# A hybrid attention and feed-forward kernel: the set-up gets a semaphore per part, its work is spread over other engines, and the planner's costs are replaced

## The reference, cut to what matters

```
x = x + attn_a(layernorm(x))     # causal, 16 heads of 16, biases, Wp
x = x + ffn(layernorm(x))        # silu(x Wg) * (x Wu), then Wd; integer weights / 127
x = x + attn_b(layernorm(x))     # sliding window of 64 keys, 16 heads; no biases
x = x + ffn(layernorm(x))        # the same ffn weights again
```

## Time and profile before

| | us |
|---|---|
| median of 3 runs | 1241.68 |
| lowest and highest | 1239.53, 1243.46 |
| the profiled execution | 1242.7 |
| its span, first to last instruction | 1240.9 |
| PE busy | 1107.1 (89%) |
| DVE busy | 830.3 (67%) |
| ACT busy | 725.8 (58%) |
| POOL busy | 385.0 (31%) |

### The profile page before, as it was taken

How to read it: one execution, slowest core, us unless ns; L and a number is a source line. 1 busy time by engine, 2 the same in 40 slices (tenths; PEclk the granted TensorE clock), 3 DMA queues, 4 the chain that set the end, 5 groups by cost and what they waited for, 6 DMA issues and landing times.

```text
span 1240.9 us, 32317 instructions
## 1 busy us (share of the span) xinstructions
PE 1107.1 (89%) x13339; PEld 670.4 (54%) x13339; DVE 830.3 (67%) x1547; ACT 725.8 (58%) x1038; POOL 385.0 (31%) x385
## 2 busy tenths in 40 slices
PE   4788888998998888999998888899899888899997
PEld 2542336765864224765685332676586422476675
DVE  7788935565687881666688893566568888256652
ACT  2257783566455777456645677456645577745653
POOL 7343223212343324202432322321233332420242
PEclk9889999999999999999999999999999999999999
DMA  7430000122223000113212200012222200011101
GB/s 281 135 134 16 11 11 23 56 74 72 75 71 109 16 11 10 46 58 103 71 36 72 100 12 11 23 56 70 72 79 71 76 16 11 11 46 52 57 19 35
DMA packets 70385, 71.64 MB, mean 58 GB/s; under 512 B 26016, under 2 KB 62304, under 8 KB 69344
## 3 DMA queue, kind: packets, MB, share of 16 engines
q1 hardware_dynamic: 70240, 69.56, 17.0%
HBM read 23.60 MB, written 8.39 MB: 26 GB/s over the span
## 4 chain that ended last, share of the span: by engine, by line
PE 67%; DVE 16%; ACT 7%; issue 4%; POOL 4%; DMA 1%; POOLq 0%; ACTq 0%; DVEq 0%
PE ring L1692 12%; PE ring L1724 7%; PE ring L1659 7%; PE ring L1725 7%; DVE peak L1254 5%; PE ring L1614 5%; ACT probs_causal L1450 4%; PE ring L1738 4%; PE ring L1743 4%; PE ring L1567 3%; DVE xn L1147 2%; PE ring L1568 2%; PE ring L1569 2%; DVE peak_c L1254 2%; POOL h_lo L1122 2%
## 5 line engine op out<-in xcount | busy, mean ns | idle before, releaser
L1254 DVE TENSOR_REDUCE peak<-ring 128x2 f32<-128x1024 f32 (+5 forms) x320 | 324.2, 1032 | 73.1 <-PE ring L1636 30.5
L1450 ACT ACTIVATE probs_causal<-ring 128x1024 f32<-128x1024 f32 (+1 forms) x320 | 286.6, 939 | 128.0 <-PE ring L1659 97.5
L1659 PE MATMUL ring<-q_st,k_st 64*64 64x192 f16 (+5 forms) x2752 | 166.0, 296 | 26.8 <-ACT probs_causal L1450 15.3
L1122 POOL TENSOR_TENSOR h_lo<-h_f,h_hi 128x512 fp32r<-128x512 f32 x96 | 122.9, 1289 | 193.0 <-ACT h_hi L1484 193.0
L1692 PE MATMUL ring<-probs_causal,V 128*32 128x512 f32 (+3 forms) x1536 | 166.5, 511 | 5.5 <-POOL probs_causal L1107 5.0
L1107 POOL TENSOR_SCALAR_AFFINE_SELECT probs_causal<-probs_causal 128x512 f32<-128x512 f32 x128 | 80.9, 635 | 281.9 <-ACT probs_causal L1450 281.7
L1724 PE MATMUL ring<-xf_hi,w_gu_sb 128*128 128x512 f32 x384 | 155.6, 405 | 7.4 <-DVE xf_lo L1154 6.6
L1113 POOL TENSOR_TENSOR onf<-osb,onf 128x512 f32<-128x512 f32 x64 | 81.6, 1276 | 241.1 <-DVE onf L1297 241.1
L1725 PE MATMUL ring<-xf_lo,w_gu_sb 128*128 128x512 f32 x384 | 150.5, 392 | 0.0
L1659 PEld LDWEIGHTS ring<-q_st,k_st 64*64 64x64 f16 x2752 | 65.9, 105 | 154.0 <-ACT probs_causal L1450 57.5
L1322 DVE SCALAR_TENSOR_TENSOR h_f<-ring,gate 128x512 f32<-128x512 f32 x96 | 65.9, 690 | 121.2 <-PE ring L1725 64.1
(11 more groups left out here) (154 smaller groups left out, 1986.4 us busy)
## 6 DMA issues: line engine op xcount, KB each, us to landing
q_st<-q_part SPq DMA_DIRECT2D x96, 128.0 KB
w_qkv<-img_qkv SPq DMA_DIRECT2D x7, 1536.0 KB, 7.7
on_lo<-onf SPq DMA_DIRECT2D x64, 128.0 KB, 2.6
k_st<-k_part SPq DMA_DIRECT2D x48, 144.0 KB, 2.1
k_st<-k_part SPq DMA_DIRECT2D x48, 128.0 KB, 2.1
y<-X SPq DMA_DIRECT2D x8, 512.0 KB, 3.0
wp_sb<-img_wp SPq DMA_DIRECT2D x7, 512.0 KB, 3.4
x_next<-in_x SPq DMA_DIRECT2D x3, 1024.0 KB, 6.2
```

Of the source, the lines that this page charges most:

```text
L1122: pool.tensor_tensor(h_lo[m][:], h_f[m][:], h_hi[m][:].bitcast(F32), ALU.subtract).then_inc(h_lo_done, 1)
L1254: dve.tensor_reduce(dst, scores, AX.X, ALU.max).then_inc(a_max, 1)
L1450: act.activation(in_banks(block[0:rows, n % slots], unit, w), heads_of(flat_of(a, e), unit, w)[0:rows], ACT.Exp, scale=back[a % 2]).then_i ...
L1659: last = pe.matmul(psum[BLOCK * m:BLOCK * m + BLOCK, r, per * n:per * n + w], keys[rows_of(r), head, first_key + BLOCK * m:first_key + BLO ...
```

## The change

The change has four parts.

1. `s_pool` is replaced by a semaphore for each part: `s_ident`, `s_rows`, `s_masks`, `s_xt_edges`, `s_onf`, and `s_v_ones` for all of the ones in `V`. POOL makes the identity first. PE starts when the identity and its bfloat16 copy are there; ACT starts at once. The rows for the stacks are made in one column and copied to 575 more. Each later user waits for its own part.
2. ACT fills the ones of `V` and the zeros of `onf` (two instructions at its start), which POOL did. The values' part of the first attention's weights is no longer scaled and split with the rest: a new event `values` splits it as soon as it has landed (ACT, POOL). The ten warm-up matmuls on PE after the first event are gone; the five ahead of it stay. The load of `bias_qk` is issued second in place of fourth.
3. POOL's residual adds (`x`) and its low parts of the gate and up weights (`gu`, last step) now wait until the second half of x is normalised.
4. The planner's costs, its delays, `LANDED`, `SOON` (0.3 to 0.15), `TABLE_LOAD` and the times at which the engines become free are replaced. The table `TIMES` gets one row more, for `values`, and is otherwise the same. All lists are made anew from this.

Cut to its core:

```
-TABLE_LOAD = 1.5
-UNITS, SOON, TURN, RELOAD = 2, 0.3, 2.0, 6.0
+TABLE_LOAD = 1.42
+UNITS, SOON, TURN, RELOAD = 2, 0.15, 2.0, 6.0
-LANDED = {('stats', 0): 0.0, ('stats', 1): 4.5, ('qkv',): 2.5, ...
+FREE = {"PE": 3.0, "ACT": 4.6, "DVE": 4.2, "POOL": 11.0, "SP": 7.5}
+LANDED = {('stats', 0): 4.7, ('stats', 1): 7.3, ('qkv',): 7.2, ...
+    "Uvalues": ((-288.91,), (-374.73,)),
...
         if kind == "B":
-            return ([("PE", 0.03 + 0.00042 * columns, 0.2), ("ACT", 0.26 + 0.00073 * w, 0.07)]
-                    + [("POOL", 0.64, 0.05)] * self.masked_on_pool(e[1], e[2]))
+            return ([("PE", 0.03 + 0.00042 * columns, 0.2), ("ACT", 0.165 + 0.00073 * w, 0.16)]
+                    + [("POOL", 0.59, 0.1)] * self.masked_on_pool(e[1], e[2]))
...
-                "T": [("PE", 0.12, 0.2), ("DVE", 0.28, 0.05), ("SP", 1.2 if self.causal else 0.6, 2.3)],
+                "T": [("PE", 0.12, 0.2), ("DVE", 0.2, 0.15), ("SP", 1.2 if self.causal else 0.6, 2.1)],
...
-            loaded = [(a, ("U", "qkv"), 2)] if self.opening else [(a, ("F", "qkv"), 0)]
+            loaded = [(a, ("U", "values"), 1)] if self.opening else [(a, ("F", "qkv"), 0)]
...
-                return [(a, ("U", "bias"), 2)]
+                return [(a, ("U", "bias"), 2), (a, ("Z", 1), 1)]
...
+        if what == "gu" and step == 2:
+            return [(("Z", 1), 1)]
...
-            pool.memset(pads[:], 0.0).then_inc(s_pool, 1)
+            pool.memset(pads[:, 0:1], 0.0).then_inc(s_rows, 1)
...
+            pool.tensor_copy(ident_b[:], ident[:]).then_inc(s_ident, 1)
             for r in range(4):
...
-                pool.affine_select(out=pads[:], in_=pads[:], compare_op=ALU.not_equal, fill=PEAK_UNIT,
-                                   base=-(8 * r + 7), pattern=[[0, KPAD // 2]], channel_multiplier=1).then_inc(s_pool, 1)
+                pool.affine_select(out=pads[:, 0:1], in_=pads[:, 0:1], compare_op=ALU.not_equal, fill=PEAK_UNIT,
+                                   base=-(8 * r + 7), pattern=[[0, 1]], channel_multiplier=1).then_inc(s_rows, 1)
+            pool.tensor_copy(pads[:, 1:KPAD // 2], pads[:, 0:1].to_broadcast([32, KPAD // 2 - 1])).then_inc(s_rows, 1)
...
-            pool.memset(V[:, ONES_BY_DVE:NT + 1], 1.0).then_inc(s_pool, 1)
-            pool.memset(onf[:], 0.0).then_inc(s_pool, 1)
...
+                elif what == "values":
+                    part, hi, lo = of_attention(0)[1], hi_of_attention()[1], lo_of_attention()[1]
+                    pool.wait_ge(s_values, 1)
+                    pool.tensor_tensor(lo, part, hi.bitcast(F32), ALU.subtract).then_inc(s_values, 1)
...
                         pool.wait_ge(s_gu[k], 2)
+                        pool.wait_ge(xn_done[1], 4)
...
                         pool.wait_ge(s_bias, 3)
+                        pool.wait_ge(xn_done[1], 4)
...
+                elif what == "values":
+                    act.wait_ge(loaded["att_a"], 16)
+                    act.activation(hi_of_attention()[1], of_attention(0)[1], ACT.Copy).then_inc(s_values, 1)
...
-            act.wait_ge(s_pool, SET_BY_POOL - 2)
+            ones = V[:, ONES_BY_DVE:NT + 1].rearrange("p t h d o -> p (t h d o)")
+            act.activation(ones, table[:, 8:9].to_broadcast([P, ones.shape[1]]), ACT.Identity, bias=1.0).then_inc(s_v_ones, 1)
+            cleared = onf[:].rearrange("p s c -> p (s c)")
+            act.activation(cleared, table[:, 8:9].to_broadcast([P, cleared.shape[1]]), ACT.Copy).then_inc(s_onf, 1)
...
-            pe.wait_ge(s_pool, SET_BY_POOL - 2)
+            pe.wait_ge(s_ident, 4)
...
             warm_up(5)
-            run(work[:1])
-            warm_up(10)
-            run(work[1:first])
+            run(work[:first])
```

More of the change, by code:

```diff
@@ L299, in streams @@
             out |= {f"Ua{h}": [("U", "stats", h)] for h in halves}
-            out |= {f"U{kind}": [("U", kind)] for kind in ("qkv", "bq", "kpre", "att_b")}
+            out |= {f"U{kind}": [("U", kind)] for kind in ("qkv", "values", "bq", "kpre", "att_b")}
             out |= {"Ub": [("U", "bias")], "Uw": [("U", "wp", n) for n in halves], "Ud": [("U", "dn")],
@@ L346, in steps @@
         if kind == "W":
[L347 removed]
+            return [("PE", 2.92, 0.2), ("DVE", 1.61 if self.causal else 0.61, 0.15)]
         if kind == "S":
[L349 removed]
+            return [("SP", 0.6 * (3, 2, 1, 1)[e[3]], 2.1)]
         if kind == "P":
             small = not self.causal and e[1] % 2
[L352 removed]
+            return [("PE", (2.92, 0.82)[small], 0.2), ("ACT", 0.3 if small else 1.02 if self.causal else 1.4, 0.15)]
@@ new lines, in steps @@
+        return {"Q": [("PE", 1.38, 0.2), ("ACT", 0.56, 0.14), ("DVE", 0.64, 0.15)],
+                "N": [("DVE", 0.6 if self.causal and e[-1] >= 4 else 0.32, 0.24)],
+                "T": [("PE", 0.12, 0.2), ("DVE", 0.2, 0.15), ("SP", 1.2 if self.causal else 0.6, 2.1)],
+                "C": [("ACT", 0.5, 0.15), ("SP", 0.6, 1.9)], "R": [("DVE", 0.16, 0.15), ("SP", 0.6, 1.7)],
+                "M": [("DVE", 0.65, 0.18), ("POOL", 1.24, 0.1)], "K": [("SP", 0.6, 2.1)],
+                "H": [("ACT", 0.53, 0.18), ("POOL", 1.25, 0.1)],
+                "O": [("PE", 1.5, 0.2)], "Y": [("DVE", 1.6, 0.15)], "X": [("DVE", 0.88, 0.15)],
+                "Z": [("ACT", 0.11, 0.14), ("DVE", 1.5, 0.2)],
+                "L": [("PE", 0.9, 0.2), ("ACT", 0.92, 0.14), ("DVE", 1.14, 0.24)],
+                "G": [("PE", 0.92, 0.2)], "E": [("ACT", 0.49, 0.14)], "I": [("DVE", 0.61, 0.13)],
+                "J": [("ACT", 0.53, 0.18), ("POOL", 1.25, 0.1)], "x": [("POOL", 2.38, 0.1)],
+                "k": [("POOL", 0.42, 0.1)]}[kind]
@@ L576, in needs_of_set_up @@
             return [(("U", "scale", 0), 4)]
+        if what == "values":
+            return [[(("D", "qkv"), 0)], []][step]
         if what in ("att_b", "kpre") and step == 0:
@@ L616, in order @@
     meant = timetable(joined)
-    free = {"PE": 0.0, "ACT": 0.0, "DVE": 0.0, "POOL": 3.0, "SP": 3.0}
+    free = dict(FREE)
     done, left, follows, known, rank = {}, {}, {}, {}, {}
```

134 lines of the change are left out of this document (66 added, 68 removed).

## The result

The change makes the kernel slower: 1275.57 us (1273.34 to 1275.91) against 1240.61, medians of four runs each, a ratio of 1.0283, interval 1.0245 to 1.0321. The profiled execution took 1275.81 us, its span is 1274.0, its mean granted clock 0.963 (before 0.977).

What follows compares the result with a forecast made beforehand. PE bounds the kernel from about 90 us; before that it mostly waits on other engines. Profiled 1242.7, less 9.5 (opening), plus 3 (sliding layers), gives 1236.2; less 1.0 to the median, 1235 us. Own range 1229 to 1241, overall 1222 to 1248.

Steps and rivals of the forecast that it cites:

- The opening up to 48 us: Start of kernel: second xn about 16.8 us, first product 27.0, first attention tile 40.5, POOL's last down-weight step 48.
- The scaling: DVE's scaling of the first attention weights: one POOL add in the way, 2.9 us; bounds 0.9 and 5.7.
- rival B: Opening: POOL's adds hold the scaling for their full 4.75 us; 1239.7 us, no change; chance 0.17.
- the rule of the Trainium skill: VectorE and GpSimd share an exclusively locked port pair; by it the released scaling would lose both adds.
- A0.0 to B0.0: Layer 0, first tile to first second pass: 40.5 to 62 us, B0.0 4.5 us earlier than before.
- The price of the check: Check after the eleventh tile in layer 0: takes 4.2 us of PE, 2 us counted against DVE.
- the point for which the prediction had 9.5: Last tiles of group 1, layer 0: 78.5 us in place of 87.97, the opening's 9.5 us gain.
- The rest of the program: After the opening: costs and SOON move events, not work; 3 us lost in sliding layers, bounds -6 and +12.
- in the causal layers ... the loss of cover and the gain cancel: 0: Causal layers: moves of one to three places both ways net 0, bounds -1 and +1 us a layer.
- The one place that was priced: Sliding layers, T4 to B4.0: three tiles and P3 fall short of cover; 0.8 us, four times, 3 us lost.
- if PE does not wait at B4.0: Sign, sliding layers: no PE wait at B4.0 would show the sliding term wrong.
- Rival C: Sliding layers' second passes: each waits 4 us more, 16 us in all; 1248 us, slower; chance 0.17.

Runs made afterwards that it cites:

- with `SOON` 0.3: Changed kernel with SOON 0.3 in place of 0.15, new costs kept; 1252.33 us, ratio 1.0082 to the kernel before.
- the run with part 4 alone: Kernel before, old set-up, with only part 4 (new costs, delays, landing times, SOON 0.15); 1290.86 us, ratio 1.0392.
- parts 1 to 3 alone: Kernel before plus parts 1 to 3, with the planner's costs, delays, landing times and SOON of before; 1234.37 us, ratio 0.9942.
- The run with the root late: Kernel with parts 1 to 3 and lists of before: ACT's H2 and C7 moved ahead of square root Z2 in four sliding layers; 1255.18 us, ratio 1.0124.
- the last run with more fillers in layer 0: New costs in layer 0 only, SOON 0.3, POOL's two waits removed from code alone; layer 0 fillers 71 in place of 43; 1233.52 us, 0.9932.

## Why the prediction was wrong

**The opening up to 48 us** was right in its path and its points in time, with terms that missed by 1 to 2 us each and cancelled, as told above. The scaling (rival B) was not held up at all: 0.86 us, since the adds wait for the value bias, which DVE makes behind the scaling. I had read the new wait as the adds' release; the later of two needs released them. So the rule of the Trainium skill (SBUF — State Buffer, "SBUF: two separate sides") was not put to the test by the scaling.

What did run beside the adds was the split of 1024 elements: 2.87 us, where it took 1.28 us with `SOON` 0.3, with POOL idle but for the first 0.2 us. The adds took 5.67 us in place of 4.75. That slowdown was in no term, and it took back part of what the scaling had saved.

**A0.0 to B0.0** failed. The price of the check, "4.2 us of PE, of which I count 2", was read from a row at full clock. It took 7.9 us at 1.2 GHz, and the tiles behind it ran at 1.2 GHz too. The opening gave 1.7 us in place of 9.5 (4.5 at the point for which the prediction had 9.5, the rest lost by the end of layer 0). With more fillers, the same lists and the clock at full, the check took 4.2 us, B0.0 came at 60.97 (forecast 62) and the opening gave 10.8 (231.1 to 220.3). So the clock is what this step left out.

**The rest of the program** is the step that failed most. "The costs and `SOON` move events, not work" and "in the causal layers ... the loss of cover and the gain cancel: 0" stand against 34.8 us in the profile and 40 in the run with part 4 alone. The runs with parts 1 to 3 alone and with part 4 alone show that the new lists carry this loss.

The one place that was priced came out near in size and not in kind. In layer 3 of the changed kernel:

```profile
579.29 0.42 PE L1650 MATMUL ring<-k_st,q_st 64*64 64x128 f16 x16 [1.32 <-DVE peak L1268]
579.72 0.31 PE L1681 MATMUL ring<-q_st,k_st 64*64 64x128 f16 x8
```

PE waited 1.3 us, where 0.8 was forecast, but ahead of the third tile, for a bank that DVE's maxima had to free. At B4.0, the second row, it did not wait, and from T4 to B4.0 passed 3.9 us against 4.6 before. By the prediction's own sign ("if PE does not wait at B4.0") the term had the wrong wait. And it was one place of hundreds, chosen because it could be seen; for the others no row gave a sign, and I took zero in the causal layers and left -6 to +12 us for the sliding ones. The run with the root late shows one pair of events that moves more than those bounds.

**Rival C** had the right sign and its argument, "the numbers in the table fit the old costs", was the right one. It got 0.17 and 4 us a layer in the sliding layers alone; the sliding ones lost 17.3 us in the profile, near its 16, and the causal ones as much again (layers 2, 4 and 6: 3.1, 9.2 and 5.2 us). That the 17.3 come of the second passes, as C has it, is not shown.

Open stay the 7 us of PE's busy time that neither clock nor waits explain, and which moves, in the sliding and in the causal layers, carry the loss.

## What to carry to other kernels

A scheduler's costs, its tie window and its table of priorities belong together: with the table as it was, other costs, another tie window in either direction or two dependencies fewer lost 12 to 129 us against the kernel before, except where the lists of nearly all layers came out as before. Whether a new table would have made the new costs pay was not tried. Compare the lists that come out first, and read the scheduler's own total: with unchanged costs it told the large losses before a run. Where the lists differ in hundreds of places, the sum over the few places that can be priced is no forecast, and its range must be as wide as such reorderings have shown. Change the set-up and the planner apart: parts 1 to 3 alone were 0.6% faster than before.

## What the runs showed that was not expected

The same matmuls of the check took 7.9 us at 1.2 GHz and 4.2 at 2.4, and 27 us of the opening ran slow after PE had waited four times, 0.35 to 0.65 us, for DVE's maxima; 371 fillers in place of 212 kept the clock at 1.00 there. In the kernel before, four such waits of 0.31 to 0.45 us (55 to 58 us) were followed by a stretch at full clock (1.00 from 58 to 66 us). In layers 1 to 7 fillers raised the clock and not the speed.

The same four `xn` instructions took 1.38 us with POOL idle (the last run with more fillers in layer 0) and 1.41 beside POOL's small constants, 2.40 beside the cast of `dn_f`, 2.79 beside the fills, and 6.88 beside two casts and a low part (`SOON` 0.3).

A0.0 came at 40.7, 37.4 and 36.9 us in three kernels with the same lists up to there. DVE waited 1.67 us, 0.60 us and not at all for the load of the second half of x, and in the first of them PE's projections ran at 1.2 GHz from 27 to 30 us. So single profiles of the opening differ by up to 4 us from this alone, and a difference of that size there shows nothing.
